# A graph kernel on one Trainium2 core: loads of the matrix issued from one queue, or half by half from two

## What is computed

```python
h = jnp.maximum(_layernorm(x, axis=-1), 0.0)
terms = [h, adj @ h]                          # Chebyshev, K = 4
for _ in range(2, 4):
    terms.append(2.0 * (adj @ terms[-1]) - terms[-2])
x = x + jnp.einsum('kni,kio->no', jnp.stack(terms), weight)
h = jnp.maximum(_layernorm(x, axis=-1), 0.0)
deg = jnp.clip(jnp.sum(adj, axis=1, keepdims=True) + 1.0, 1.0, None)
h_neigh = (adj @ h + h) / deg
out = jax.nn.relu(jnp.concatenate([h, h_neigh], axis=1) @ W + b)
x = x + out / jnp.maximum(jnp.linalg.norm(out, axis=1, keepdims=True), L2_EPS)
```

## Time and profile before

| | us |
|---|---|
| median of three runs | 2939.23 |
| the three runs | 2846.58, 2948.15, 2939.23 |
| span of the profiled execution | 2906.5 |
| PE busy in it | 2229.9 |
| DVE busy | 1637.0 |
| ACT busy | 729.8 |

### The profile page before, as it was taken

One profiled execution on the slowest core, in us unless ns is written; L12 is line 12 of the kernel. 1 busy time (PEld: TensorE's weight loads), 2 busy tenths in 40 slices (PEclk: granted clock), 3 DMA queues, 4 the chain that ended last, 5 costly groups with the idle time before them and its releaser, 6 DMA issues.

```text
span 2906.5 us, 20534 instructions
## 1 busy us (share of the span) xinstructions
PE 2229.9 (77%) x6792; PEld 946.0 (33%) x6792; DVE 1637.0 (56%) x1204; ACT 729.8 (25%) x2243; POOL 35.8 (1%) x73
## 2 busy tenths in 40 slices
PE   2566877798888889979888878778776786777666
PEld 0122333343343334434333333333232232322222
DVE  5555665556545556555455566555545455577666
ACT  4556656666555553000000000000000000000000
POOL 0000000000000000000000000000000000001001
PEclk9788889888999999999999999889888888889877
DMA  9999999999999999999999999999999999999996
GB/s 220 238 239 259 275 266 265 252 266 277 229 228 234 232 231 219 230 228 235 235 235 232 233 220 231 233 223 226 223 222 223 227 229 236 246 309 283 231 229 142
DMA packets 428333, 689.56 MB, mean 237 GB/s; under 512 B 56514, under 2 KB 130242, under 8 KB 428226
## 3 DMA queue, kind: packets, MB, share of 16 engines
q1 hardware_dynamic: 425344, 685.95, 105.2%
q0 software_dynamic: 2048, 2.10, 0.3%
q10 hardware_dynamic: 834, 0.20, 0.0%
HBM read 685.97 MB, written 2.10 MB: 237 GB/s over the span
## 4 chain that ended last, share of the span: by engine, by line
SPq 71%; DMA 10%; PE 9%; issue 4%; ACT 3%; DVE 2%; POOL 0%; DVEq 0%
SPq L315 71%; DMA ring<-in_adj_dram 10%; PE ps_pair L721 6%; ACT ring L370 3%; PE ps_single L727 2%; DVE ring L577 2%; SPq L304 0%; PE ps_lin L666 0%; PE ps_lin L669 0%; PE ps_lin L681 0%; PE ps_tr L685 0%; DVE vec L573 0%; PE ps_lin L682 0%; POOL out_dram L330 0%; PE ps_lin L672 0%
## 5 line engine op out<-in xcount | busy, mean ns | idle before, releaser
L577 DVE STREAM_TRANSPOSE ring<-ring 128x2048 f32<-128x2048 f32 x640 | 1431.6, 2283 | 1073.6 <-DMA ring<-in_adj_dram 713.3
L721 PE MATMUL ps_pair<-ring,vec 128*128 128x512 f32 x2880 | 1356.9, 629 | 263.0 <-DVE ring L577 246.4
L721 PEld LDWEIGHTS ps_pair<-ring,vec 128*128 128x128 f32 x2880 | 570.1, 202 | 1017.1 <-issue 869.2
L727 PE MATMUL ps_single<-ring,vec 128*64 128x512 f32 x2240 | 623.1, 697 | 329.5 <-DVE ring L577 326.2
L370 ACT ACTIVATE ring<-ring 128x512 f32<-128x512 f32 x1024 | 627.9, 614 | 416.0 <-DMA ring<-in_adj_dram 416.0
L727 PEld LDWEIGHTS ps_single<-ring,vec 128*64 128x64 f32 x2240 | 168.0, 156 | 707.8 <-issue 474.6
L397 ACT ACTIVATE sum_s<-ps_single 128x512 f32<-128x512 f32 x64 | 37.7, 589 | 634.9 <-PE ps_pair L721 461.2
L370 ACT ACTIVATION_READ_ACCUMULATOR ring<-ring 128x1 f32 x1024 | 191.3, 187 | 0.0
L399 ACT ACTIVATE sum_p<-ps_pair 128x512 f32<-128x512 f32 x45 | 26.5, 590 | 499.5 <-PE ps_pair L721 499.5
L348 ACT ACTIVATE stat<-stat,eps 128x4 f32<-128x4 f32 (+1 forms) x20 | 6.0, 299 | 312.5 <-DVE stat L519 310.1
L573 DVE STREAM_TRANSPOSE vec<-ring 128x512 f32<-128x512 f32 x40 | 25.1, 682 | 91.5 <-issue 81.5
(11 more groups left out here) (94 smaller groups left out, 542.0 us busy)
## 6 DMA issues: line engine op xcount, KB each, us to landing
ring<-in_adj_dram SPq DMA_DIRECT2D x2320, 256.0 KB, 13.7
ring<-in_adj_dram SPq DMA_DIRECT2D x192, 192.0 KB, 12.8
ring<-in_adj_dram SPq DMA_DIRECT2D x192, 128.0 KB, 9.3
ring<-in_adj_dram SPq DMA_DIRECT2D x192, 64.0 KB, 6.0
res<-in_x_dram SPq DMA_DIRECT2D x8, 256.0 KB, 5.9
out_dram<-vec POOLq DMA_DIRECT2D x64, 32.0 KB, 7.1
tmp<-in_L_gnn_weight_dram ACTq DMA_DIRECT2D x2, 64.0 KB
row_sums<-in_L_gnn_W_dram ACTq DMA_DIRECT2D x2, 32.0 KB
```

The lines of the kernel that those rows point to most:

```text
L577: nc.vector.transpose(blocks, blocks).then_inc(s_turned, 1)
L721: last = nc.tensor.matmul(ps_pair[n % 2][:], vec[:, CB * J + c, :, :], moving, start=(k == pair_at[0] and c == 0), stop=(k == pair_at[-1] ...
L727: last = nc.tensor.matmul(ps_single[n % 2][half:half + F, :], vec[:, CB * J + c, single_slot, :], moving, start=(k == single_at[0] and c < 2),
```

## The change

The loads of `ring` are divided by the quarter `a` that they fill. Quarters 0 and 1 (partitions 0 to 63) stay on SP's queue, at the same places. Quarters 2 and 3 (partitions 64 to 127) are issued by ACT, in a function `load_high(done)` that issues the high halves of all strips whose buffer is free once `done` units are done, waiting on `s_unit` for each. It is called at the start (the first four strips), ahead of each sum of the first sweep, at the start of each row, ahead of each evacuation, and ahead of the square root. `s_strip` becomes two groups of six semaphores, `s_low` and `s_high`, with half the count each, and ACT and DVE wait for both.

```diff
@@ SyncE
                 for ar in range(Q):
-                    for a in range(Q):
+                    for a in (0, 1):
...
-                        sp.dma_start(dst, src).then_inc(s_strip[i % NSEM], 16)
+                        sp.dma_start(dst, src).then_inc(s_low[i % NSEM], 16)
@@ ScalarE
+            begun = [0]
+
+            def load_high(done):
+
+                while begun[0] < len(strips) and strip_start[places[begun[0]][1]] <= done:
+                    i = begun[0]
+                    n, J0, w, _ = strips[i]
+                    if places[i][1] > 0:
+                        act.wait_ge(s_unit, strip_start[places[i][1]])
+                    for ar in range(Q):
+                        for a in (2, 3):
+                            col = a * QN + J0 * UC
+                            src = adj_v[ar, :, CB * rows[n].C:CB * rows[n].C + CB, col:col + w * UC]
+                            dst = strip_of(i)[32 * a:32 * a + 32, ar:G:Q, :]
+                            act.dma_start(dst, src).then_inc(s_high[i % NSEM], 16)
+                    begun[0] += 1
...
+            load_high(0)
             act.wait_ge(s_zero, 4)
@@ sum_rows(i)
-                act.wait_ge(s_strip[i % NSEM], 16 * Q * Q * (i // NSEM + 1))
+                if i:
+                    load_high(strip_start[i - 1])
+                act.wait_ge(s_low[i % NSEM], 8 * Q * Q * (i // NSEM + 1))
+                act.wait_ge(s_high[i % NSEM], 8 * Q * Q * (i // NSEM + 1))
@@ the rows of ScalarE
                     sum_rows(first + 1)
+                load_high(row_start[n])
...
                 if n - 1 in late_at:
+                    load_high(late_at[n - 1])
...
                     sum_rows(first_strip[n + 1])
+                load_high(row_start[n + 1])
                 act.wait_ge(s_unit, row_start[n + 1])
...
                 if n in root_rows:
+                    load_high(min(row_start[n + 1] + 2, first_need.get(n, n_units)))
@@ VectorE
-                dve.wait_ge(s_strip[i % NSEM], 16 * Q * Q * (i // NSEM + 1))
+                dve.wait_ge(s_low[i % NSEM], 8 * Q * Q * (i // NSEM + 1))
+                dve.wait_ge(s_high[i % NSEM], 8 * Q * Q * (i // NSEM + 1))
```

More of the change, by code:

```diff
@@ L275, in cheb_sage_kernel @@
         s_wready = sem("weights_ready")
-        s_strip = [sem(f"strip_loaded{i}") for i in range(NSEM)]
+        s_low = [sem(f"strip_low_loaded{i}") for i in range(NSEM)]
+        s_high = [sem(f"strip_high_loaded{i}") for i in range(NSEM)]
         s_turned = sem("units_turned")
```

## The result

| | before | after |
|---|---|---|
| median of the runs, us | 2929.4 (4 runs) | 2664.9 (4 runs, 2659.9 to 2677.9) |
| ratio | | 0.9305, 95% interval 0.918 to 0.943 |
| span of the profiled execution | 2906.5 | 2675.9 |

The ratio compares only the fast runs of both kernels; the two medians alone would give 0.910. The change makes the kernel faster, by 7% on the ratio. The forecast was 2530 in a range of 2330 to 2945, that is 14%. The direction came true, and of the gain a good half: 231 us of 406, from the span of 2906.5 (2675.9 measured, 2500 forecast).

The account below looks back on a forecast made before the run. Loads, held by the DMA transfer, were taken to bound the kernel. Start and stages 70 + 970 + 490 + 660 + 310 = 2500, plus 33 is 2533; predicted 2530 us, ratio 0.861, range 2330 to 2945.

Parts of the forecast that it names:

- Bound: Whole kernel before: loads are the limit, their issue held by the transfer, 2320 loads of 256 KB at 225 to 265 GB/s.
- Rate: Loads from two queues, a half of the partitions each: 324 GB/s, the best stretch, against 232 for no gain.
- rival B: Loads: no gain in rate, two queues share the same 16 busy engines; 2903 to 2945 us, within 2%; chance 0.15.
- Start: Before the first unit: ACT issues 32 loads ahead of its first square; first unit at about 70 us for 64.
- Sweep 1: First sweep: 970 us for 1065, near the lower end of the loop with epilogues, 957 to 1008.
- The loop of the forecast: First sweep, over two strips: ACT's issues, sum, transpose, PE's strip, handing over, evacuation; 28.5 to 30.1 us.
- Sweep 2: Second sweep: PE is the bound with 479 us busy; 490 with the narrow strips, for 551.
- Sweep 3: Third sweep and partial rows of 4: 660 us for 867, PE's 650; late evacuations cost nothing at four-block strips.
- Last rows: End of the kernel: loads 272 us at 324 GB/s plus a 28 us tail, taken as 310 for 359.
- The 33 us on top: Whole time: the runs' median lies 33 us above the span of 2906.5; the same 33 added to 2500.
- A: Loads: half the gain, ACT and SP seldom full together; 245 to 264 GB/s, 2733 to 2850 us; chance 0.14.
- C: ACT, held in its full queue, hands over late while the rate stays near 232; slower, 3220 us; chance 0.11.

Follow-up runs that it names:

- all_three: The changed kernel with ACT's issues behind the sum, the row's last strip issued behind the evacuation, and the short start together; 2372.2 us, 0.822 of the kernel before.
- after_sum: The changed kernel, but ACT issues the high half of strip i+2 behind the sum of strip i, not ahead; 2582.5 us, 0.892 of the kernel before.
- evac_first: The changed kernel, but the last strip's loads that stood ahead of a row's evacuation are issued behind it; 2471.2 us, 0.854 of the kernel before.

## Why the prediction came out as it did

**Bound: right.** The loads were the bound, held by the transfer and not by the issue. Taking them down moved the time, and the only-loads kernel in the old order runs at 224 GB/s with nothing beside it.

**Rate: right for the bare loads, too high for the kernel.** 324 GB/s was taken from the best stretch. The only-loads kernel gives 350, and rival B, no gain in rate, fell: 350 against 227 for the same two queues without the division. In the kernel after it is some 300 per busy share, and in the first sweep of `all_three`, with the engines busy throughout, 284. The sum did not feel it, since only the start and the last rows were taken from the loads' time. The step from the earlier trace rows to the change is partly luck. That busy engines can move more is true, but what let one queue reach 324 for 50 us is not shown: 16 of its 64 loads are of 192 KB, not "of the same kind", and the bare loads in the same order never pass 243 GB/s in a slice of the page.

**Start: the size off by 6.** PE's first unit starts at 76.0 us against 70; the loads of `x` behind those of ACT were left out.

**Sweep 1: the mechanism right, the size off.** The loop was named with its parts, and it is the bound, as `after_sum` shows: 1039 us from the first unit to the last evacuation, against 970. The chain of that stretch, as shares of it (the view itself cuts the line off):

```profile
by line: ACT ring L392 30.7%; PE ps_pair L748 25.2%; ACTq L351 14.3%; PE ps_single L754 12.3%; DVE ring L604 5.1%; PE ps_lin L693 2.6%; issue 2.4%; PE ps_lin L696 2.3%; PE ps_lin L695 1.1%; PE ps_tr L712 0.9%; PE ps_xt L645 0.8%; PE ps_sing
```

The loop of the forecast takes two strips a round, so 32 rounds. Of its terms the sums are as forecast (30.7% of 1039 is 319 us, for 32 x 9.9 = 317). Three terms are too small. PE's units have 390 us for 365. ACT's issues have 149 for 122: one strip's eight took 4.0 us as by SP's price of 0.47, but some groups on the chain stand ahead of an evacuation and not ahead of a sum. And the epilogues, `ps_lin` and `ps_tr`, have 72 for 48. Together that is 76 us; 1039 exceeds the lower end of the forecast's loop, 957, by 82 (I had taken 970). The fifteen epilogues of the sweep took 3.2 to 7.8 us, for the 3 that I took.

A part of this is PE's clock. By windows of the kernel after, the stretch with the epilogue shown above:

```profile
443.00:463.00 20.00, 19.93 (x68) 10.04 (x70) 16.98 (x12) 9.13 (x29) 0.00 (x0) 0.60 0.58 187
```

At a granted clock of 0.60, that is for the most part at the lower of its two levels (1.2 and 2.4 GHz), a single unit takes 3.6 to 3.7 us, for the 1.8 that I took, and the epilogue 454.44 - 446.75 = 7.7; PE had been idle for 6.7 us before. Four pair units took 16.0 us at a clock of 0.88 (411 to 426 us), for 13.9. (In the kernel before an epilogue took 4.4 us, from 517.0 to 521.4 us; the 3 us were low for that, too.)

**Sweep 2: the number right, by luck.** 497 us against 490. I had PE busy for 479 and next to no waits; it is busy for 466 and waits 31 us for evacuations, which I had put at nothing. `evac_first` takes 455.

**Sweep 3: the step that failed.** 749 against 660. "I cost it at nothing where strips are four blocks wide": I asked whether the loads run dry while ACT is late, and they do not, but by then they are not the bound. PE is, and PE waits for the evacuation itself behind eight or sixteen issues. That is 4 us at each row where the queue has room and up to 12 where it has not. Of PE's 223 us of waits for `sum_s` and `sum_p`, 107 lie in this stretch, and `evac_first` takes 110 us from it, more than the 89 that were missing. The same sentence said where to look: what stands behind the waiting instruction was named, the evacuation and then PE, and only its price was put against the wrong resource.

**Last rows: the number right, by luck.** 315 against 310. I took the loads as the bound there; their share is 0.83, and 71 of PE's 223 us of waits lie here. `evac_first` takes 284.

The stages' errors, 6 + 69 + 7 + 89 + 5 = 176, are the whole of 2675.9 - 2500. The 33 us on top were wrong too: the time of this profiled execution is 2677.9, 2 above its span, so the 33 were for the most part the distance from one execution of before to the median of others, not work around the span.

**The rivals.** A (245 to 264 GB/s, since the queues are seldom full together) gives the mean rate of the profile, 258, but not the time: its 2733 to 2850 lie above the 2665. Its cause is the smaller part. From 350 to 258, the share of the engines fell from 1.06 to 0.87, as PE frees buffers late; the rest is 300 per busy share for 330 (350 / 1.06), and there A may be right. C did not happen here; with the halves mixed its time came out, but not its working.

**What would show it.** Of the signs listed, DMA share and ACT's 3.8 to 5.4 us, PE's part of the chain, SP's waits (1798 us) and sweep 2's PE share (466 / 496 = 94%) came true. So did DVE's waits: 328 us for ACT's sums in the first sweep, while its waits for loads fell from 713 to 176 us in the whole kernel. The rows of the first sweep in 58 to 62 us did not (1045 / 16 = 65). The rate of 290 was reached only per busy share. PE waiting for evacuations was listed as a sign of C, together with ACT's issues at 1 us and more; both are there in part in the third sweep.

## What to carry to other kernels

If the DMA engines are busy all the time and still move fewer bytes in one stretch than in another, ask which parts of the destination and of the source are in use at the same time, and measure it with a kernel that only loads. When loads go to a computing engine's queue, put each issue where nothing on the path stands behind it: behind the evacuation and the sum, not ahead, since eight issues are 4 us even with an empty queue. And once a change takes the bound away, price its side effects against the next bound (here PE's waits), not against the one that it removes.

## What the runs showed of the hardware

- Loads into 32 partitions each, with no computing beside them: 224 GB/s from one queue in the order of quarters 0, 1, 2, 3; 239 in the order 0, 2, 1, 3; 227 from two queues that each mix the halves; 350 from two queues with a half each (of the partitions, and with them of the matrix's columns). Beside the computing, two queues with a half each gave 284 at a DMA share of 1.04.
- The same halves from SP's and POOL's queue: 264 GB/s, with POOL's queue at half as many packets for the same bytes.
- An issue of a load on ACT takes 0.45 us and a gap of 0.03, about as on SP (0.43 and 0.04). With the queue full it took 1.3 to 2.5 us. Issues also ran while ACT's earlier activations were still being worked off:

```profile
405.01 0.28 ACTq L351
405.29 0.24 ACT ring L392
405.53 0.09 ACTq L351
405.62 0.52 ACT ring L392
```

  So the issues behind a sum are in part hidden under it, and those that wait for PE ahead of a sum are not.
